# Where the output stores of one chunk are issued on ScalarE's queue

## The reference

```python
x = x + _L0_attn_ref(_layernorm(x), Wk, bk, Wv, bv, Wq, bq)   # FFTs, a cumulative sum, a norm
x = x + _L0_ffn_ref(_layernorm(x), w_in, w_out, w1, w2, wg, we, gb, eb)
```

```python
def _L0_ffn_ref(x, w_in, w_out, w1, w2, wg, we, gb, eb):
    ...
    shared = _swiglu(flat @ w_in.T) @ w_out.T
    g_probs = jax.nn.softmax(flat @ wg.T + gb, axis=-1)
    g_idx = jnp.argmax(g_probs, axis=-1)
    e_logits = flat @ we.T + eb
    ...
    topv, topi = jax.lax.top_k(p_expert, TOP_K)
    w_se = jnp.zeros((S, NUM_EXPERTS), x.dtype).at[jnp.arange(S)[:, None], topi].add(topv)
    h = _swiglu(flat @ w1.T)
    routed = jnp.zeros_like(shared)
    for e in range(NUM_EXPERTS):
        routed = routed + h * w_se[:, e:e + 1] @ w2[e].T
    return (shared + routed).reshape(Bs, Ts, C)
```

## Time and profile before

| | us |
|---|---|
| median of 3 runs | 4661.73 (4661.42 to 4663.81) |
| the profiled execution, its own time | 4662.21 |
| its span on the slowest core, core 5 | 4661.2 |
| spans of the eight cores | 4627.3 to 4661.2 |
| PE busy, of the span | 3839.0 (82%) |
| ACT busy, of the span | 515.1 (11%) |
| DVE busy, of the span | 1091.5 (23%) |

### The profile page before, as it was taken

The page is one execution under the profiler, slowest core; times in us unless marked ns, Lnnn a source line. Parts: engine busy times, 40 slices in busy tenths (PEclk is TensorE's granted clock), DMA queues, the critical chain, the costliest instruction groups (busy, mean ns, idle before and its releaser), DMA issues.

```text
span 4661.2 us, 46789 instructions; the slowest of 8 cores (4627.3 to 4661.2 us)
## 1 busy us (share of the span) xinstructions
PE 3839.0 (82%) x17976; PEld 1706.6 (37%) x17976; DVE 1091.5 (23%) x2177; ACT 515.1 (11%) x789; POOL 123.3 (3%) x234
## 2 busy tenths in 40 slices
PE   4568623149995789999979999979999996999999
PEld 1223201014442334444434444434444443444444
DVE  0150311024453311222221122231122223111111
ACT  1110111014443101000010100011000001110000
POOL 0000000000000000000000000000000000000000
PEclk8769856579997899999989999989999998999999
DMA  5440699981212134222212322223132221212111
GB/s 91 79 120 0 70 117 118 119 119 55 64 55 73 46 103 134 84 91 82 77 55 76 128 82 82 82 77 109 41 120 104 93 88 44 91 59 113 73 73 73
DMA packets 71322, 391.17 MB, mean 84 GB/s; under 512 B 10160, under 2 KB 10160, under 8 KB 59328
## 3 DMA queue, kind: packets, MB, share of 16 engines
q0 software_dynamic: 24480, 253.88, 23.0%
q1 hardware_dynamic: 41024, 117.46, 7.9%
q10 hardware_dynamic: 5600, 16.84, 0.9%
HBM read 423.81 MB, written 88.08 MB: 110 GB/s over the span
## 4 chain that ended last, share of the span: by engine, by line
PE 76%; DMA 7%; another core or an unknown queue 7%; DVE 5%; issue 2%; ACT 2%; DVEq 1%; ACTq 0%; POOL 0%; POOLq 0%; SPq 0%
PE ps_r L1106 19%; PE ps_tb L1106 19%; PE ps_a L1030 4%; PE ps_tb L1030 4%; PE ps_r L1037 4%; PE ps_b L1037 4%; PE ps_r L1073 2%; PE ps_kv L355 2%; PE ps_tb L1073 2%; PE ps_id L355 2%; DMA w<-w2s 2%; PE ps_id L511 2%; PE ps_q L355 2%; DMA xf<-x 1%
## 5 line engine op out<-in xcount | busy, mean ns | idle before, releaser
L1106 PE MATMUL ps_r<-w,hsT 128*128 128x512 bf16 x4096 | 913.5, 381 | 34.8 <-DMA w<-w2s 34.8
L1106 PE MATMUL ps_tb<-w,hsT 128*128 128x512 bf16 x4096 | 904.9, 379 | 0.0
L1106 PEld LDWEIGHTS ps_r<-w,hsT 128*128 128x128 bf16 x4096 | 402.6, 98 | 525.4 <-issue 48.1
L1106 PEld LDWEIGHTS ps_tb<-w,hsT 128*128 128x128 bf16 x4096 | 400.7, 98 | 483.3
L355 PE MATMUL ps_kv<-wtk_b,xT_b 128*128 128x512 bf16 x512 | 133.0, 419 | 325.4 <-ACT xT_b L352 325.4
L1030 PE MATMUL ps_a<-hiT,wab 128*128 128x512 bf16 x1024 | 248.1, 398 | 136.3 <-DMA wab<-wabs 126.9
L1114 DVE SCALAR_TENSOR_TENSOR acc<-ps_tb,wse,acc 128x1024 f32<-128x1024 f32 x128 | 164.3, 1283 | 719.8 <-PE ps_tb L1106 719.8
L1114 DVE SCALAR_TENSOR_TENSOR acc<-ps_r,wse,acc 128x1024 f32<-128x1024 f32 x128 | 164.3, 1283 | 670.3 <-PE ps_r L1106 670.3
L1037 PE MATMUL ps_r<-hiT,wab 128*128 128x512 bf16 x1024 | 231.4, 379 | 1.1 <-DMA wab<-wabs 1.1
L1030 PE MATMUL ps_tb<-hiT,wab 128*128 128x512 bf16 x1024 | 231.4, 379 | 0.3 <-DMA wab<-wabs 0.3
L1037 PE MATMUL ps_b<-hiT,wab 128*128 128x512 bf16 x1024 | 231.5, 379 | 0.0
(11 more groups left out here) (203 smaller groups left out, 2625.5 us busy)
## 6 DMA issues: line engine op xcount, KB each, us to landing
w<-w2s POOLq DMA_DIRECT2D x72, 2048.0 KB, 13.1
w2s<-w2T POOLq DMA_DIRECT2D x8, 4096.0 KB, 379.4
wab<-wabs POOLq DMA_DIRECT2D x128, 256.0 KB, 3.1
wab<-wabs SPq DMA_DIRECT2D x128, 256.0 KB, 2.6
xf<-xp SPq DMA_DIRECT2D x32, 512.0 KB, 4.8
xf<-x SPq DMA_DIRECT2D x32, 512.0 KB, 4.1
x1s<-x_sb SPq DMA_DIRECT2D x32, 512.0 KB, 4.9
x1t<-x1s SPq DMA_DIRECT2D x32, 512.0 KB, 9.3
```

Source lines behind the costliest of these rows:

```text
L1106: mi = PE.matmul(pr[:, 512 * h:512 * (h + 1)], hsT[:, hc * CH + i * 128: hc * CH + (i + 1) * 128], w2_b[bi][:, hc * D + 512 * h: hc * D + ...
```

## The change

The stores of a chunk are no longer issued in round e = 7. They are noted in a list, and ACT issues all eight in a row in the next chunk, behind the copy of the gate logits and ahead of the exponentials of the gate. For the last chunk, which has no next one, they are issued after the loop. Each store keeps its own wait for its tile. Nothing else changes.

```diff
@@ -996,6 +997,11 @@
                 ACT.copy(glog[:, :], ps_b[:, 0:10 * TPC]).then_inc(sc_gl, 1)
+                for (tgt, cc0, ii) in pend_st:
+                    ACT.wait_ge(sv_acc, tgt)
+                    ACT.dma_start(out_t4[cc0, ii], acc[:, ii * D:(ii + 1) * D]
+                                  ).then_inc(s_out, 16)
+                pend_st.clear()
                 for i in range(TPC):
                     s1_gate(i)
@@ -1118,12 +1124,15 @@
                         if e == NE - 1:
-                            ACT.wait_ge(sv_acc, n_r)
-                            ACT.dma_start(out_t4[c, i], acc[:, i * D:(i + 1) * D]
-                                          ).then_inc(s_out, 16)
+                            pend_st.append((n_r, c, i))
                 if c + 1 < NCH:
                     wout_load(c + 1)
                 DVE.engine_nop().then_inc(sv_fin, 1)
+            for (tgt, cc0, ii) in pend_st:
+                ACT.wait_ge(sv_acc, tgt)
+                ACT.dma_start(out_t4[cc0, ii], acc[:, ii * D:(ii + 1) * D]
+                              ).then_inc(s_out, 16)
+            pend_st.clear()
             SP.wait_ge(s_out, 128 * NCH)
```

More of the change, by code:

```diff
@@ L826, in build_nc @@
             g_done = {}
+            pend_st = []
             gx_ln = {}
```

## The result

The changed kernel takes 4686.31 us in the median of 11 runs, the one before 4667.89 us in 11 runs beside it. The ratio is 1.0041, with a 95% interval of 1.0029 to 1.0052: about 19 us slower, where "the same, 4670" was forecast, and above the stated range (4663 to 4678). The comparison leaves out the executions, of both kernels, in which the clock of one half of the chip was lower; the medians of all runs above contain them.

A forecast was written before the change was run, and what follows sets the result against it. PE was taken to wait at each chunk's start for the serial gate chain on DVE and ACT. Three boundaries at 2.79 us add 8.4 to 4662.2, giving 4670.6 (4670.1 by the median); predicted 4670 us, 8-in-10 range 4663 to 4678.

The forecast's parts named there:

- Where the time would go: PE's wait before block 2 grows from 31.3 to about 34 us at three boundaries, through a late first exponential: 8.4 us.
- what one issue takes when eight stand in a row: ACT's issues between `glog` copy and first exponential: 0.34, twice 0.38, five times 0.54; 3.80 us, 4.61 with gaps.
- upper bound of 0.98: Six of ACT's eight issues at 0.98 us each, from an SP store at 100% busy DMA engines: 16.8 us in all.
- The room: ACT's idle time between the end of the `glog` copy and the first exponential, hiding 1.82 us of the issues.
- issues slow down against their own traffic: ACT's third to eighth issue take 0.73 us each: 12.3 us over three boundaries, 4674 us; chance 0.27.
- ACT is held until descriptors are taken: ACT's eighth issue ends only after seven stores are drained: 36.8 us over three boundaries, 4699 us; chance 0.06.
- half must drain: Milder case of ACT held in its row of issues: only half must drain first, 19 us over three boundaries, 4681 us.
- the issues hide: Wait and issue cost ACT some 0.2 us, hidden before the first exponential: 0 us, 4662; chance 0.11, shared with favourable clock.
- faster: Gains of 0.6 us from the freed ACT and up to 5 from the clock, together within 0.2%; chance beyond that 0.04.
- the clock: PE's granted clock at the three boundaries may fall otherwise: at most 5 us either way, added as 0.
- The transfers cost nothing: Moved stores are over by about 3911, before PE's load starts at 3935; a collision is costed at nothing.
- The stores removed from round e = 7 give nothing: 24 of 32 stores leave a place where ACT idles 53.78 us; three boundaries could give 0.6 us, taken as 0.

## Why the prediction was wrong

- *Where the time would go*: right. The loss is in PE's wait before block 2 at three boundaries, by way of the first exponential; chunk 0 (31.2 us of wait, 32.3 before) and the tail show nothing of it. The shift passed through undiminished (18.8 us of late exponentials, block 2 later by 18.5).
- *The step that failed* is the term "what one issue takes when eight stand in a row". I took 0.34, twice 0.38 and five times 0.54, 3.80 us. Measured: 0.34, 0.40, 0.74, 1.16, 1.48, 0.94, 1.20 and 1.21, 7.45 us. The third to eighth average 1.12 us, above even my upper bound of 0.98. With gaps and start the exponential came 6.24 us late, not 2.79.
- *Why the bound was too low*: I took each row of SP's issues as if the pace of an issue were a property of the instruction, loaded or not. The rows of before were rows of two or four. The fourth of four on a starting program (0.54 on most cores) is not yet the steady pace. Also, 0.98 was no upper bound even of my own rows: the earlier trace rows have a third issue of 1.19 us on core 0. The half-size stores and the packets between two issues show that the pace is that of the engines.
- *The room*: I had 1.82 us from the end of the copy. The issue doesn't wait for the copy to end; from the first issue to the old exponential there were 1.98 us. A small error in the other direction.
- *Rival "issues slow down against their own traffic"*: the right mechanism at too low a price, 0.73 for 1.12 us.
- *Rival "ACT is held until descriptors are taken"*: for eight equal stores this is the closest picture, and I gave it 0.06. ACT came free when 714 of the 1024 rows had started. Its price for "half must drain", 19 us, is the measured loss, but by luck: more than half had to start, and the 4 MB moved in some 11 us instead of the 16.1 that I took. The row that I held against it was true (a store of 4096 KB takes 0.38 to 0.44 us) and said nothing of a row of issues. As a limit on the amount of data this rival still fails, since large stores in a row are held no longer than small ones. The rule from "Perfetto Trace Analysis", "DMA Instruction — HWDGE (DVE, Sync)", of the Trainium skill, that the sequencer is occupied until all of the issue's descriptors are generated, fits the occupied sequencer. Taken alone it doesn't foresee that 2048 KB take 1.18 us where 512 KB take 1.16.
- *Rival "the issues hide"* and the gains named under *faster*: refuted by the same rows; the clock shows no part in it, since the late exponentials alone give the loss. (The profiled spans differ by 21.8 us, of which 2.6 lie ahead of the first chunk's gate, where nothing was changed.)
- *The transfers cost nothing*: right. One store of 4 MB and eight from SP both give ratios of 1.00.
- *The stores removed from round e = 7 give nothing*: in line with the runs; no gain is seen in any kernel with moved stores.
- *The chances*: 0.36 for slower was too little, since the sum stood close under the edge of 9.3 us with its least known term multiplied by three.

## What to carry to other kernels

Don't put a row of DMA issues on a compute engine ahead of the first link of a serial chain; spread them into idle gaps, give them to an engine that nobody waits for, or make one transfer of them. Price such a row not by a single issue but, from the third or fourth on, by the time that the DMA engines need for 128 of its rows: here 1.29 us with rows of 4 KB, 0.69 with rows of 2 KB. And before moving work around a chain that PE waits for, look whether the chain can leave the path: that made the kernel 2.7% faster here, while the moved stores made it 0.4% slower.

## What the runs showed of the hardware

- Issues on one queue with no pause: 0.34, 0.40, 0.74, then about 1.2 us, from ACT and from SP alike. With the gap of 0.09 that is 1.29 us per issue with rows of 4 KB. With rows of 2 KB it is 0.69, from the sixth issue on. The size of the transfer hardly matters (1.16 us for 512 KB, 1.18 for 2048 KB). With five microseconds between issues it is 0.338, and SP's issue 6.5 us behind a load of 4096 KB took 0.32 with that load still under way. Between the ends of two such issues about 128 rows start, of either length and whatever the issue brings. Why it is that number, and why the issue's own size doesn't count, stays open.
- At some boundaries, the last above all, single issues took 1.3 to 1.7 us in place of 1.2, and one 2.03. The next ones were often shorter (1.48, then 0.94), and the row of the changed kernel ended 8.06 us after its start, as at the second boundary (8.08). This was seen and not explained, and neither was the 2.03 to 2.30 us of the first moved store between the gate tiles.
- A DMA issue on ACT started 0.07 us behind the start of the compute instruction ahead of it, 0.16 us before that one's end.
